# Reciprocal roots of the head norms by logarithm and exponential on ScalarE, with the ramp in a new order

## The reference, cut to what matters

```
h = modulate(rmsnorm(x), shift, scale)
q, k, v = split(h @ qkv_w.T)             # 16 heads of 8 features
q = q_norm_w * q * rsqrt(mean(q*q) + 1e-6)     # per token and head
k = k_norm_w * k * rsqrt(mean(k*k) + 1e-6)
q, k = rotate(q, pos), rotate(k, pos)    # first 6 of the 8 features
o = softmax(q @ k.T * 8**-0.5) @ v
x = x + gate * (o @ proj_w.T + proj_b)
x = x + gate2 * swiglu(modulate(rmsnorm(x)))
```

## Time and profile before

| | |
|---|---|
| median of 3 runs | 199.43 us (199.38 to 200.79) |
| the profiled execution's own time | 200.87 us |
| its span (first to last instruction) | 199.0 us |
| PE, DVE, ACT, POOL busy | 89%, 82%, 65%, 71% |

### The profile page before, as it was taken

One profiled execution on the slowest core, in us unless ns is written; L12 is line 12 of the kernel. 1 busy time (PEld: TensorE's weight loads), 2 busy tenths in 40 slices (PEclk: granted clock), 3 DMA queues, 4 the chain that ended last, 5 costly groups with the idle time before them and its releaser, 6 DMA issues.

```text
span 199.0 us, 6095 instructions
## 1 busy us (share of the span) xinstructions
PE 177.7 (89%) x2039; PEld 141.8 (71%) x2039; DVE 163.4 (82%) x495; ACT 129.2 (65%) x379; POOL 141.2 (71%) x333
## 2 busy tenths in 40 slices
PE   1588887998999999999999998999999799998954
PEld 1445555775768777778887887999998577986742
DVE  5699988898898989899887546678889799999861
ACT  1377698678677687777658576454431559999630
POOL 8889888898989898898980194435556646586641
PEclk9999999999999999999999999999999999999987
DMA  5964006900000000000000000000000000011111
GB/s 99 295 167 188 2 5 230 405 5 3 3 0 5 3 3 3 3 0 5 3 0 3 3 2 3 0 2 0 3 0 3 0 3 0 0 33 53 53 52 30
DMA packets 10428, 8.32 MB, mean 42 GB/s; under 512 B 3105, under 2 KB 9886, under 8 KB 9886
## 3 DMA queue, kind: packets, MB, share of 16 engines
q1 hardware_dynamic: 7006, 7.25, 10.9%
q10 hardware_dynamic: 3392, 0.68, 1.7%
HBM read 6.86 MB, written 1.07 MB: 40 GB/s over the span
## 4 chain that ended last, share of the span: by engine, by line
PE 45%; DVE 17%; issue 6%; ACT 3%; POOL 3%; POOLq 0%; ACTq 0%; DVEq 0%
PE bank L1946 5%; PE bank L2051 5%; PE bank L891 5%; PE bank L892 5%; DVE qkpad L1661 5%; PE bank L903 4%; PE bank L1955 3%; PE bank L936 2%; PE bank L957 2%; PE bank L2025 2%; PE bank L1996 1%; PE bank L1983 1%; PE bank L1971 1%; PE bank L1027 1%; POOL rstd L528 1%
## 5 line engine op out<-in xcount | busy, mean ns | idle before, releaser
L1661 DVE TENSOR_REDUCE qkpad<-bank 128x4 f32<-128x512 f32 x64 | 41.0, 683 | 8.4 <-PE bank L1946 7.5
L1352 ACT ACTIVATE probs<-bank 128x512 f32<-128x512 f32 x64 | 34.6, 595 | 17.6 <-PE bank L1955 16.7
L1946 PE MATMUL bank<-kBD,qTs 32*128 32x256 f32 x224 | 31.7, 399 | 3.8 <-ACT probs L1352 1.6
L1955 PE MATMUL bank<-qTm,kBD 32*128 32x128 f32 x448 | 32.5, 283 | 0.0
L1955 PEld LDWEIGHTS bank<-qTm,kBD 32*128 32x128 f32 x448 | 27.1, 186 | 0.0
L1946 PEld LDWEIGHTS bank<-kBD,qTs 32*128 32x128 f32 x224 | 19.7, 184 | 9.6 <-DVE qkpad L1661 5.6
L596 ACT ACTIVATE th<-bank 128x256 f32<-128x256 f32 x24 | 9.3, 387 | 14.7 <-PE bank L892 11.9
L2051 PE MATMUL bank<-probs,vpad 128*32 128x128 f32 x512 | 17.3, 276 | 0.0
L2051 PEld LDWEIGHTS bank<-probs,vpad 128*32 128x32 f32 x512 | 12.9, 109 | 5.6 <-ACT probs L1352 5.5
L2025 PE MATMUL bank<-qkvT,hT 128*128 128x384 f32 x32 | 15.3, 572 | 0.5 <-ACT hT L1369 0.5
L1996 PE MATMUL bank<-ident,qkpad 128*128 128x128 f32 x96 | 14.2, 277 | 1.1 <-POOL qkpad L1235 0.9
(11 more groups left out here) (253 smaller groups left out, 526.9 us busy)
## 6 DMA issues: line engine op xcount, KB each, us to landing
gate<-in_cond_dram SPq DMA_DIRECT2D x1, 1024.0 KB, 4.7
x<-gate_rows SPq DMA_DIRECT2D x1, 1024.0 KB, 4.7
y<-gate_rows SPq DMA_DIRECT2D x1, 1024.0 KB, 6.8
res<-gate_rows SPq DMA_DIRECT2D x1, 1024.0 KB, 10.2
out_dram<-res SPq DMA_DIRECT2D x7, 128.0 KB, 1.8
xin<-in_x_dram ACTq DMA_DIRECT2D x2, 256.0 KB, 5.4
xin<-in_x_dram SPq DMA_DIRECT2D x1, 512.0 KB, 5.4
ada_n<-in_L_cond_ada_w_dram SPq DMA_DIRECT2D x1, 256.0 KB, 5.7
```

What stands on the lines that cost most here:

```text
L1352: q.activation(probs[2 * r + i][:, :, :, :].rearrange("p f a t -> p (f a t)"), exp_bank(t, r, i)[:, :], ACT.Exp, scale=SCALE).then_inc(s_p, 1)
L1661: q.tensor_reduce(out_, score_bank(b, r, i)[:, :].rearrange("p (f a t) -> p f a t", f=2, a=2), X_AXIS, ALU.max, negate=True).then_inc(s_ma ...
L1946: last = q.matmul(bank[S_BANK[i]][:, f * 2 * T:(f + 1) * 2 * T], qTs[b % 2][rows, f, :], kBD[b % NKB][rows, f, :, :].rearrange("p a t -> p ...
L1955: last = q.matmul(bank[E_BANK[i]][:, (2 * f + k) * T:(2 * f + k + 1) * T], kBD[t % NKB][rows, f, k, :], qTm[t % 2][rows, f, :], start=True ...
```

## The change

In place of seed and two steps, the root comes as exp(-0.5 ln(m)) from ACT, with one refining step behind it. DVE no longer makes a seed; it splits the range of the sum into a lower and an upper part (`ranges`, two instructions). ACT makes `ns` (Identity), then the logarithm of both parts (`nl`, 128 x 128) and after it their exponential (`ne`). POOL, for the first pair DVE, multiplies the two parts and takes one step: five instructions on POOL for ten, four on DVE for seven. The factor 1.5 that the seed's steps left in `qkw` goes.

```
+            def ranges(b):
                 j = b // 2
                 v.wait_ge(s_ss, b + 1)
+                q.tensor_scalar(nr[j % 2][:, 0, :, :], nms[j % 2][:, :, :], SPLIT, None, ALU.min)
+                q.tensor_scalar(nr[j % 2][:, 1, :, :], nms[j % 2][:, :, :], DH / SPLIT, float(DH), ALU.mult, ALU.max).then_inc(s_nr, 1)
...
+            def logs_of_heads(b):
+                a.wait_ge(s_nr, j + 1)
+                if j == 2:
+                    a.wait_ge(h_newton, EARLY_NEWT)
+                wait(a, s_newton, NEWT * (j - 2))
+                q.activation(ns[j % 2][:, :, :], nms[j % 2][:, :, :], ACT.Identity, bias=half_eps[:, 0:1], scale=0.5 / DH)
+                q.activation(nl[:, :, :, :], nr[j % 2][:, :, :, :], ACT.Ln, bias=eps[:, 0:1], scale=1.0 / DH).then_inc(s_ln, 1)
+            def roots_of_heads(b):
+                a.wait_ge(s_ln, j + 1)
+                q.activation(ne[j % 2][:, :, :, :], nl[:, :, :, :], ACT.Exp, scale=-0.5).then_inc(s_sd, 1)
...
             def rsqrt_of_heads(b):          # POOL; early_rsqrt on DVE likewise
+                g.wait_ge(s_sd, j + 1)
+                q.tensor_tensor(y_, e_[:, 0, :, :], e_[:, 1, :, :], ALU.mult).then_inc(s_newton, 1)
                 q.tensor_tensor(t_, y_, y_, ALU.mult)
                 q.tensor_tensor(t_, t_, s_, ALU.mult)
                 q.tensor_tensor(t_, three_halves[:, :, :], t_, ALU.subtract)
                 q.tensor_tensor(y_, y_, t_, ALU.mult)
-                (five more: the second step)
```

More of the change, by code:

```diff
@@ L1471, in _ @@
             values(3)
+            weights(P_W1, bank[P_BANK][:, 0:FC * 128], w1T[:, :], 1.0)
+            logs_of_heads(3)
+            roots_of_heads(3)
             input_normed(4)
             input_normed(5)
+            keys_and_queries(1)
             modulated_input(4)
-            weights(P_W1, bank[P_BANK][:, 0:FC * 128], w1T[:, :], 1.0)
+            weights(P_W3, bank[P_BANK][:, 0:FC * 128], w3T[:, :], 1.0)
             squares(4)
@@ L1528, in _ @@
                 spread_of(t - 2)
+                if t == B - 5:
+                    silu_input()
                 if t == B - 4:
@@ L1591, in _ @@
             assert n == V_MOD
[L1592 removed]
+            count(q.tensor_copy(qkw[:, :, :].rearrange("p s d -> p (s d)"), bank[4][:, 64:64 + 2 * DH]))
             assert n == V_QKW
@@ L1724, in square_sums @@
                 v.wait_ge(s_sq, b + 1)
+                wait(v, s_sd, b // 2 - 1)
                 q.tensor_reduce(nms[b // 2 % 2][:, b % 2, :], sq[b % 2][:, :, :], X_AXIS, ALU.add).then_inc(s_ss, 1)
-            def seeds(b):
+            def ranges(b):
                 if not is_seq(b) or b % 2 == 0:
@@ L1768, in _ @@
             rope_part(v, q, 0, rope_v)
+            mean_squares(slice(HEAD_B, MID_B), A_MID, V_MSMID)
             square_sums(0)
-            mean_squares(slice(HEAD_B, MID_B), A_MID, V_MSMID)
             masks()
             square_sums(1)
-            seeds(1)
+            ranges(1)
             early_rsqrt()
@@ L1780, in _ @@
             queries(0)
-            seeds(3)
+            square_sums(3)
+            ranges(3)
             rowmax(0, 0, 0)
@@ L1793, in _ @@
             square_sums(5)
-            seeds(5)
+            ranges(5)
             b_fed, b_first, b_rest, gate_, gated_ = blocks_vector(v)
@@ L1807, in _ @@
                 square_sums(t + 6)
-                seeds(t + 6)
+                ranges(t + 6)
                 if B - 6 <= t < B - 3:
@@ L2073, in _ @@
             prepare_modulations()
+            queries_and_keys(0)
             prepare_hidden(w1_n)
-            input_turned(4)
-            queries_and_keys(0)
-            queries_keys_values(4)
-            input_turned(5)
             e.wait_ge(s_kq, 1)
```

111 lines of the change are left out of this document (53 added, 58 removed).

## The result

The changed kernel takes 201.96 us (median of 8 runs, 201.75 to 206.86) against 199.87 for the kernel before in the same session (199.37 to 200.85): ratio 1.0092, 95% interval 1.0058 to 1.0126. It is slower by about 2 us. Three of its eight runs lay at 205.2 to 206.9 with a granted clock (TensorE's mean clock over the run, 1 being full speed) of 0.967 to 0.974 and are left out of the ratio; the five others lie at 201.75 to 202.01, with 201.84 in the middle.

A forecast was written before the change was run, and what follows sets the result against it. PE was taken to bound the loop, a chain across engines the ramp. Ramp +2.3, round 0 +0.15 and loop -1.1 gave +1.4 us on the median 199.43: 200.8 us, range 198.4 to 202.4.

The forecast's parts named there:

- Distance of the halves: Ramp, PE: second half of the scores of sequence 1 starts 3.77 us behind the first, in place of 1.43.
- `kBD` of sequence 1: Ramp, ACT: starts at 23.15 against 23.13 before, so no gain; bounds -0.4 and +0.8.
- Ramp: Stretch before round 0: costs 2.3 us, bounds 1.3 and 3.0, with PE's and ACT's chains agreeing.
- Table load behind `angles()`: Ramp, ACT: delays `sq` and `qk` of sequence 0 by 0.7 us at most; its scores still gain 0.4 to 0.9.
- Round 0: First round of the loop: costs PE 0.15 us more.
- Loop: Waits of 2.2 us on PE go; even rounds 2, 4, 6, 8 cost 0.2 each, 0.8 in all.
- Round 10: Table load of 1.28 us on ACT for the late Tanh: 0.2 us on PE plus 0.1 for `hT`.
- POOL ends where it did: Even rounds: POOL waits for ACT's exponential and ends its five instructions 5.4 us in, against 5.53 before.
- The drain: Table loads on ACT: 1.3 us each by the row, without the skill page's extra drain of about 1.38.
- (2): Rival, clearly slower: ramp costs 3.0 and the loop gives little, +2.7 us, 202.1; chance 0.28.
- (1): Rival, not slower: ramp costs 1.3, loop gives 2.2 back, -0.6 us, 198.8; chance 0.2.
- (3): Rival: Ln and Exp need two tables, so each even round has two loads, 215 us; chance 0.02.

The follow-up runs named there:

- Experiment 5: Changed kernel with the products of sequences 4 and 5 back ahead of the scores of sequence 1, ACT and POOL following: 198.21 us, ratio 0.9937.
- experiment 1: Changed kernel with the second half of the scores of sequence 1 ahead of the q, k, v product of sequence 5 on PE: 205.16 us, ratio 1.0242.
- experiment 8: Kernel before with a table load behind `angles()`, `silu_input` in round 11 and `style` in round 12: 201.68 us, ratio 1.008.
- experiment 11: The kernel of 7, unchanged, profiled in an execution at full clock: 197.85 us.
- experiment 3: Changed kernel's ramp order, late Tanh and table load behind `angles()`, with the old seed and two steps: 203.32 us, ratio 1.0161.
- 7: Experiment 5 with ACT's logarithm and exponential in the loop moved behind the `hT` of sequence t + 6: 198.08 us, ratio 0.9933.
- 2: Changed kernel's arithmetic and tables, with each program of the ramp in the order of the kernel before: 202.2 us, ratio 1.0093.
- 6: Changed kernel with `first_modulations` moved behind `input_turned(2)` on PE: 202.64 us, ratio 1.0133.
- 9: Experiment 5 with `first_modulations` moved behind `input_turned(2)` on PE: 199.62 us, ratio 1.0016.
- the execution of 428 us: Profiled execution, not used, of the changed kernel with ACT's loop logarithm and exponential behind the `hT` of sequence t + 6; that kernel's ratio 1.0084.

## Why the prediction was right, and where not

The forecast was 200.8 us with a range of 198.4 to 202.4, "within 1%" the likeliest; measured were 201.96 and a ratio of 1.0092. The mechanism was right and its size too small: the ramp was put at 2.3 us and cost 2.93. That the ratio stayed within 1% was close and in part luck: its interval reaches 1.0126, and at full clock it is 201.85 to 199.55, 1.2%. Point by point:

- **Distance of the halves, 3.77.** Measured 4.08. Of the steps, the scores' 1.06, the 0.70 to `hT` and the 0.52 behind it came as said; `sq` started 0.95 behind the product instead of 0.84, and PE held 0.84 for the second product instead of 0.65.
- **`kBD` of sequence 1 at 23.15, "no gain".** 23.54, within its bounds (22.7 to 23.9). ACT waited 1.64 for `nr`, as feared, whose first part took DVE 0.80. Experiment 5 shows what is possible with the same arithmetic: 22.57. This term is 0.38 of the miss; the middle of its bounds, 23.3, would have left 0.24 of it.
- **Ramp 2.3 (1.3 to 3.0).** 2.93: 0.38 at the first half, 2.65 between the halves (for 2.34), 0.10 given back behind them. This is the term that was mis-sized, by 0.6. That ACT's chain moves by the same amount was right (2.97) and experiment 1 shows that it binds on its own.
- **Table load behind `angles()`, a delay of 0.7 at most.** The first read of the first product came 0.63 later than before (12.92 against 12.29), and in experiment 8, where order and arithmetic are the old ones, 0.77. The gain of 0.4 to 0.9 for the scores of sequence 0 all the same was right: 0.74.
- **Round 0, +0.15.** 0.18.
- **Loop, -2.2 + 0.8.** Rounds 1 to 9 gave -1.63 for -1.4: the even rounds cost 0.15 each and not 0.2, and by experiment 11 it is the wait for `hT`. The wait of round 3 went, but experiment 3 shows that the longer ramp alone takes it away too, and experiment 5 that the arithmetic alone does. The prediction gave it to the arithmetic only.
- **Round 10, +0.3; round 11, nothing.** 0.37 and 0.32. The load of 1.28 was priced on ACT and through `hT`, not through DVE, whose row maxima stand in order behind `yg`: 1.63 idle there, 0.41 on PE in the next round.
- **POOL ends where it did.** Its five steps end 5.4 us into the round, as worked out, behind an idle time of 2.09 (1 to 2 was said).
- **The drain.** ACT went on 0.01 to 0.02 us behind each load (11.62 and 1.28, then 12.92; 95.11 and 1.28, then 96.40). The Trainium skill (ScalarE: Activation LUTs, What ACT_TABLE_LOAD costs) has a drain of 1.38 beside the load; no load here shows one, so the row was the right guide.
- **The sum.** +1.4 was worked out, +2.17 measured up to round 12. That the profiled span of 200.1 lies so near the forecast 200.4 is luck: the sum was 0.8 too small, and the profiled execution of before, to which it was added, had lost 1.1 us of clock at its end. The prediction saw that execution to be 1.44 above the median and did not ask why. Of the rivals, (2) names what happened in the ramp (3.0), at 202.1, with a loop that gives little, which was wrong; (1) and (3) did not occur; experiment 5 shows that the same arithmetic, with the products ahead of the scores, does reach a time such as (1) had (198.2 against 198.8).

## What to carry to other kernels

When a change brings new arithmetic and a new order of a start-up, price them apart: here everything that experiment 5 keeps of the change (the arithmetic, the late Tanh, the early transpositions of the modulations) was worth 1.4 us, and the order of the products with what follows it on ACT cost 3.65, and the sum hid both. In a chain over several engines count how often the path crosses from one to the other between two steps that belong together; here a product whose input came behind ACT's reading of the last one cost the whole round trip, 2.65 us. And if the first dense work is followed by a gap, look at the sizes of like instructions behind it before looking for waits.

## What the hardware showed that was not expected

- TensorE's speed in the ramp depended on a swap of two items. Where PE went on at once behind its first products, pairs of products took 0.91 from 15 us on (changed kernel, experiments 5, 7 and 11). Where it stood there for 0.45 to 0.73 us, for `vpad`, they took 1.39 to 1.65 until 23 to 26 us (2, 6, 9). The granted clock in the records stays at 1.00 in windows of that stretch (15 to 20 and 20 to 25 in 2 and 9), so only the durations show it. It also stands at 1.00 over the first four products, which in every one of these executions took 2.72 to 2.90: the slow pace is the one that all start with, and what differs is when it ends. It is no strict rule: in 8 PE stood for 0.45 us too and had full speed at 15.43 in the profiled execution (200.6), while four of its six runs were 1.1 us slower. What decides between the two is left open.
- Another loss does show in the granted clock: 0.50, the lower level of 1.2 GHz, in 37 to 39 behind an idle stretch of 2.13 us (1) and in 19 to 25 behind one of 1.40 (3), with matmuls of nearly twice the duration. In 1 round 1 starts at 39.89 in place of 38.68 although the exponentials came 0.22 earlier, so the clock cost some 1.4 us on top of the wait. An idle stretch ahead is no sure sign either way. In the profile of 7 the clock was 0.66 in 25 to 30 though PE's longest wait since 15 us had been 0.69, and a wait of 1.18 stands ahead of the last input transposition in both the kernel before, which ran slow behind it, and the changed kernel, which did not.
- A table load on ACT took 1.28 us in every trace, and in all but that of the execution of 428 us the next instruction followed within 0.02 us of its end.
